# A state-space scan in rounds: another order of work on PE, VectorE and ScalarE, with y's two halves a round apart

## The reference

```python
A = -jnp.exp(A_log)
def step(hst, ins):
    dt_t, B_t, C_t, x_t = ins
    dA = jnp.exp(dt_t[:, :, None] * A)
    hst = hst * dA + (dt_t * x_t)[:, :, None] * B_t[:, None, :]
    y_t = jnp.einsum('bds,bs->bd', hst, C_t)
    return (hst, y_t)
```

## Time and profile before

| | us |
|---|---|
| median of 3 runs | 7119.47 (7112.84 to 7120.07) |
| profiled execution, its own time | 7115.03 |
| span of the profiled execution | 7113.3 |
| PE busy | 6393.6 (90%) |
| VectorE busy | 4188.9 (59%) |
| ScalarE busy | 4613.4 (65%) |
| GpSimd busy | 3331.1 (47%) |
| mean granted clock of PE | 0.932 |

### The profile page before, as it was taken

One profiled execution on the slowest core, in us unless ns is written; L12 is line 12 of the kernel. 1 busy time (PEld: TensorE's weight loads), 2 busy tenths in 40 slices (PEclk: granted clock), 3 DMA queues, 4 the chain that ended last, 5 costly groups with the idle time before them and its releaser, 6 DMA issues. The chain is left out here.

```text
span 7113.3 us, 205317 instructions
## 1 busy us (share of the span) xinstructions
PE 6393.6 (90%) x85792; PEld 3192.1 (45%) x85792; DVE 4188.9 (59%) x6974; ACT 4613.4 (65%) x9618; POOL 3331.1 (47%) x2816
## 2 busy tenths in 40 slices
PE   6888679999999999999999999979899999978988
PEld 3444434444444444444444444434355445444544
DVE  2555556666666666666666666655344445445554
ACT  3555478888888888888888888852244345345554
POOL 0011156666666666666666666640033223224432
PEclk8999879999999999999999999989999999989999
DMA  6555522222222222222222222235200000010000
GB/s 192 150 142 138 159 68 59 59 58 58 65 60 58 59 58 65 60 59 58 59 59 66 59 59 59 58 123 201 95 7 7 10 7 10 4 35 13 10 13 7
DMA packets 596363, 459.87 MB, mean 65 GB/s; under 512 B 449728, under 2 KB 504640, under 8 KB 577280
## 3 DMA queue, kind: packets, MB, share of 16 engines
q1 hardware_dynamic: 594408, 444.73, 21.5%
q10 hardware_dynamic: 1048, 2.16, 0.1%
HBM read 301.29 MB, written 145.49 MB: 63 GB/s over the span
## 5 line engine op out<-in xcount | busy, mean ns | idle before, releaser
L1472 POOL TENSOR_TENSOR s_dec<-s_hs,s_dec 128x512 f32<-128x512 f32 x2040 | 2561.5, 1281 | 1212.7 <-DVE s_hs L1512 791.9
L1393 ACT ACTIVATE s_dec<-s_pa 128x512 f32<-128x512 f32 x4096 | 2268.9, 618 | 403.8 <-PE s_pa L1246 403.6
L1501 DVE TENSOR_TENSOR s_pA<-s_pA,s_dec 128x512 f32<-128x512 f32 x2040 | 1393.0, 694 | 830.3 <-ACT s_hs L1399 563.9
L1512 DVE TENSOR_TENSOR s_hs<-s_pB,s_dec 128x512 f32<-128x512 f32 x2040 | 1330.9, 684 | 338.1 <-PE s_py L1283 236.8
L1283 PE MATMUL s_py<-s_hs,s_cz 128*32 128x256 f32 x16384 | 1392.4, 418 | 0.0
L1399 ACT COPY s_hs<-s_pA 128x512 f32<-128x512 f32 x2048 | 1210.3, 599 | 205.0 <-PE s_pA L1256 201.8
L1292 PE MATMUL s_py<-s_still 128*32 128x512 bf16 x15848 | 1243.2, 386 | 0.0
L1246 PE MATMUL s_pa<-s_dl,s_al 18*128 18x64 bf16 x32768 | 958.9, 192 | 79.7 <-DMA s_dl<-D 48.6
L1256 PE MATMUL s_pA<-az 18*128 18x256 bf16 x4096 | 778.7, 285 | 180.5 <-DVE s_pA L1501 176.5
L1256 PE MATMUL s_pB<-az 18*128 18x256 bf16 x4096 | 826.5, 283 | 3.5 <-DMA az<-U 3.5
L2067 POOL TENSOR_TENSOR t_prob<-t_prob,t_rinv 128x512 f32<-128x512 f32 x512 | 528.7, 1039 | 508.5 <-DVE t_rinv L2440 508.5
(11 more groups left out here) (260 smaller groups left out, 6395.2 us busy)
## 6 DMA issues: line engine op xcount, KB each, us to landing
s_dl<-D SPq DMA_DIRECT2D x512, 144.0 KB
az<-U SPq DMA_DIRECT2D x1024, 72.0 KB
az<-B SPq DMA_DIRECT2D x1024, 36.0 KB
D<-p_dp SPq DMA_DIRECT2D x64, 384.0 KB, 5.8
U<-p_up SPq DMA_DIRECT2D x60, 384.0 KB, 6.3
B<-p_bz SPq DMA_DIRECT2D x144, 128.0 KB, 2.5
SZ<-p_sz SPq DMA_DIRECT2D x16, 1024.0 KB, 4.0
SK<-p_skip SPq DMA_DIRECT2D x16, 1024.0 KB, 5.8
```

Source lines behind the costliest of these rows:

```text
L1393: act.activation(dec[w][:].rearrange("p k i t d -> p (k i t) d")[:, :, DS * q + d:DS * q + d + 8], pa[:, bank, :].rearrange("p (d c) -> p ...
L1472: pool.tensor_tensor(m, two(hs[k][:, (x + 1) % 2, :]), m, ALU.mult).then_inc(m_done, 1)
L1501: dve.tensor_tensor(state, state, of_chunk(k, x), ALU.mult).then_inc(mul, 1)
L1512: dve.tensor_tensor(out, two(pB[:, k - 2, :]), of_chunk(k, x), ALU.add).then_inc(added, 1)
```

## The change

PE's `body`, VectorE's `body` and one wait of ScalarE are rewritten.

- VectorE does, in a normal round, `times` 0, `plus` 3 of the round before, `times` 1, `plus` 2. In x = 0 and 8 `plus` 3 of the round before comes first, ahead of `dec_ready`. One `plus` 3 stands behind the last body.
- PE, in a normal round: `to_a` 0; y of round n-2, half 1; `keep_warm`; `to_b` 3 of this round; `produce` w = 0 with `to_a` 1 beside it; y of round n-1, half 0; `keep_warm`; `produce` w = 1 with `to_b` 2 of the next round beside it. The halves of y are a round apart. x = 0, 8 and x = 1, 9 have orders of their own. `beside` is now called ahead of the products i = 2 and i = 4, and not at the start and at i = 3.
- `keep_warm` writes to `py` only, is called 31 times a body, and still makes two sets.
- ScalarE's `copy_a` of chunk 0 waits also for `y_mm` of 2n-2.

```diff
--- before.py
+++ after.py
@@ -1235,12 +1235,10 @@
             def _(pe):
                 def adt(p, w, banks, beside=None):
 
-                    if beside:
-                        beside(0)
                     wait(pe, taken, 2 * p - 1)
                     for i in range(8):
-                        if beside and i == 3:
-                            beside(1)
+                        if beside and i in (2, 4):
+                            beside(i // 2 - 1)
                         for e in range(2):
                             q, d = 2 * (w[1] % 2) + e, 8 * (w[1] // 2) + i
                             mm = pe.matmul(pa[:, banks[e], DS * i:DS * (i + 1)],
@@ -1285,11 +1283,11 @@
                                        start=(x == 0 and v == 0), stop=(x == BODY - 1), skip_group_check=True)
                     mm.then_inc(y_mm, 1)
 
-                def keep_warm(onto):
+                def keep_warm():
 
                     for _ in range(2):
                         for k in range(CH):
-                            pe.matmul(onto[QR * k:QR * (k + 1), :], still[:, W:W + QR], still[:, 0:W],
+                            pe.matmul(py[QR * k:QR * (k + 1), :], still[:, W:W + QR], still[:, 0:W],
                                       start=False, stop=False, skip_group_check=True)
 
                 def turn_y(p, G, banks):
@@ -1315,58 +1313,77 @@
                     for x in range(BODY):
                         n = BODY * G + x
                         more = not (last and x >= TB)
-                        late = x == 1
-                        before = (x - 1) % BODY
-                        has = not (head and x == 0)
                         ahead = not (last and x == BODY - 1)
-
-                        def to_a0(v):
-                            to_a(n, x, 0, v)
+                        old = (x - 1) % BODY
+
+                        def to_a1(v):
+                            to_a(n, x, 1, v)
 
                         def to_b2(v):
-                            if late and v == 0:
-                                wait(pe, added, 2 * n + 1)
-                                keep_warm(pB[:, 0, :])
                             to_b(n + 1, (x + 1) % BODY, G + (x + 1) // BODY, 2, v)
 
-                        if more and x % TB == 0:
-                            produce(G, x, 0, head, turn, None)
-                            if has:
-                                keep_warm(py)
-                            to_a0(0)
-                            to_a0(1)
-                        elif more:
-                            produce(G, x, 0, head, turn, to_a0)
-                        else:
-                            to_a0(0)
-                            to_a0(1)
-                        for v in range(2):
-                            to_a(n, x, 1, v)
-                        if has and not late:
-                            if x == 9:
-                                wait(pe, c_filled, 2 * G + 2)
-                            y(n - 1, before, 0)
-                            keep_warm(py)
-                        if more:
-                            produce(G, x, 1, head, turn, to_b2)
-                        elif ahead:
+                        def to_b3():
+                            if n:
+                                for v in range(2):
+                                    to_b(n, x, G, 3, v)
+
+                        def make(w, beside):
+                            if more:
+                                produce(G, x, w, head, turn, beside)
+                            elif beside:
+                                beside(0)
+                                beside(1)
+
+                        if x % TB == 0:
+                            if n:
+                                y(n - 2, (x - 2) % BODY, 1)
+                                keep_warm()
+                            to_b3()
+                            make(0, None)
+                            if n:
+                                y(n - 1, old, 0)
+                                keep_warm()
+                            to_a(n, x, 0, 0)
+                            to_a(n, x, 0, 1)
+                            make(1, None)
+                            to_a1(0)
+                            to_a1(1)
+                            if n:
+                                y(n - 1, old, 1)
                             to_b2(0)
                             to_b2(1)
-                        if has and not late:
-                            y(n - 1, before, 1)
-                            if x:
-                                keep_warm(py)
-                        if ahead:
-                            if late:
-                                wait(pe, added, 2 * n + 2)
-                                keep_warm(pB[:, 1, :])
-                            for v in range(2):
-                                to_b(n + 1, (x + 1) % BODY, G + (x + 1) // BODY, 3, v)
-                        if late:
-                            wait(pe, ytok_done, G)
-                            wait(pe, c_filled, 2 * G + 1)
-                            for v in range(2):
-                                y(n - 1, before, v)
+                        elif x % TB == 1:
+                            to_a(n, x, 0, 0)
+                            to_a(n, x, 0, 1)
+                            make(0, None)
+                            to_b3()
+                            if x == 9:
+                                keep_warm()
+                            to_a1(0)
+                            to_a1(1)
+                            if x == 1:
+                                make(1, None)
+                                wait(pe, ytok_done, G)
+                                wait(pe, c_filled, 2 * G + 1)
+                                y(n - 1, old, 0)
+                                keep_warm()
+                                to_b2(0)
+                                to_b2(1)
+                            else:
+                                wait(pe, c_filled, 2 * G + 2)
+                                y(n - 1, old, 0)
+                                keep_warm()
+                                make(1, to_b2)
+                        else:
+                            to_a(n, x, 0, 0)
+                            to_a(n, x, 0, 1)
+                            y(n - 2, (x - 2) % BODY, 1)
+                            keep_warm()
+                            to_b3()
+                            make(0, to_a1)
+                            y(n - 1, old, 0)
+                            keep_warm()
+                            make(1, to_b2 if ahead else None)
                         if x == 2 and not head:
                             turn_y(15 + 33 * G + 6, G, [(12 + e) % BANKS for e in range(2)])
 
@@ -1380,6 +1397,7 @@
                     for v in range(2):
                         to_b(0, 0, 0, k, v)
                 bodies(body)
+                y(BODY * ALL - 2, BODY - 2, 1)
                 y(BODY * ALL - 1, BODY - 1, 0)
                 y(BODY * ALL - 1, BODY - 1, 1)
                 p = 15 + 33 * (ALL - 1) + 17
@@ -1395,6 +1413,8 @@
                         pa[:, bank, :].rearrange("p (d c) -> p c d", d=8), ACT.Exp).then_inc(taken, 1)
 
                 def copy_a(n, x, k):
+                    if k == 0:
+                        wait(act, y_mm, 2 * n - 2)
                     wait(act, bu_a, 2 * n + k + 1)
                     act.copy(hs[k][:, x % 2, :], pA[:, k, :]).then_inc(copied, 1)
 
@@ -1500,15 +1520,17 @@
                         state = two(pA[:, k, :])
                         dve.tensor_tensor(state, state, of_chunk(k, x), ALU.mult).then_inc(mul, 1)
 
-                def plus(n, made, x, k, first):
+                def plus(n, k):
+                    G, x = n // BODY, n % BODY
+                    made = 2 * (n - G // BODIES)
                     wait(dve, bu_b, 2 * n + k - 1)
                     if k == 2:
                         wait(dve, y_mm, 2 * n - 2)
                     out = two(hs[k][:, x % 2, :])
-                    if first:
+                    if n % (BODY * BODIES) == 0:
                         dve.tensor_copy(out, two(pB[:, k - 2, :])).then_inc(added, 1)
                     else:
-                        wait(dve, m_done, made + 2 * x + k - 3)
+                        wait(dve, m_done, made + k - 3)
                         dve.tensor_tensor(out, two(pB[:, k - 2, :]), of_chunk(k, x), ALU.add).then_inc(added, 1)
 
                 def take_y(G):
@@ -1521,15 +1543,19 @@
                     for x in range(BODY):
                         n = BODY * G + x
                         start = first and x == 0
+                        if x % TB == 0 and n:
+                            plus(n - 1, 3)
                         dec_ready(dve, G, x, head)
-                        for k in range(2):
-                            times(n, x, k, start)
+                        times(n, x, 0, start)
+                        if x % TB:
```

(6 more changed lines are left out.)

## The result

| | before | after |
|---|---|---|
| median of the runs | 7119.47 us (3 runs) | 7222.0 us (7219.52 to 7226.81, 3 runs) |
| ratio | | 1.015 (95% interval 1.0136 to 1.0164) |
| span of the profiled execution | 7113.3 us | 7217.7 us |
| mean granted clock of PE | 0.932 | 0.897 |
| a body of the scan | 59.57 us | 61.25 us |

The account below looks back on a forecast made before the run. PE's own work was taken to bound normal rounds, with irregular rounds adding waits and half clock. A body of 18.81 + 10.74 + 8 x 3.15 = 54.75 us against 59.57 saves 303: 7115 - 303 = 6812 us, range 6690 to 7020.

Parts of the forecast that it names:

- the sum: Scan body: 18.81 + 10.74 + 8 x 3.15 = 54.75 us against 59.57, 303 us less in 63 bodies.
- rival 2: PE's clock still falls in x=1: 6.8 us of half clock, 3.2 us a body, total 7014 us; chance 0.20.
- PE's blocks, the normal round: PE's two product blocks in a normal scan round take 0.58 and 0.57 us, the round 3.15, without waits for other engines.
- if no product passed another: PE's matmuls never reorder: each block some 0.02 us longer, 30 us in all, total 6842 us.
- The boundary, the turn, the body: Scan: x=7 to 10 takes 10.74 us, x=15 to 4 18.81, a whole body 54.75.
- The clock: PE's granted clock in the scan was forecast near 1.0.
- the new thin stretch in x=1: PE waits about 1.2 us in 2.5; judged nearer to busy 5.31 of 6.60 (no fall) than 1.52 of 3.50 (fall).
- Rival 4: Slower: idle 0.9 us before turn_y keeps the clock low into x=3 to 5; +76 us, 7191 us; chance 0.05.

Follow-up runs that it names:

- e4: The kernel before with only VectorE's new order, PE and ScalarE unchanged: 7103.7 us, 0.9987 of before.
- e7: e1 with VectorE's order of before (times 0, times 1, plus 2, plus 3): 6914.7 us, 0.9716 of before.
- e8: e1 with one set of zero-weight products instead of two behind y's older half in normal rounds: 6644.7 us, 0.9344 of before.
- e1: The changed kernel with three more keep_warm calls: in x=0 and 8, in x=1, ahead of the turn of y: 6783.6 us, 0.9534 of before.
- e5: The kernel before with two more keep_warm calls in x=1, ahead of and behind to_a 1: 6917.9 us, 0.972 of before.
- e2: The changed kernel with only e1's added keep_warm call in x=0 and 8: 6946.8 us, 0.9763 of before.
- e6: The kernel before without the keep_warm call behind y's second half in x=8: 7117.6 us, 1.0005 of before.
- e10: e1 without its added keep_warm call ahead of the turn of y: 6791.6 us, 0.9548 of before.
- e3: The changed kernel with only e1's added keep_warm calls in x=1 and ahead of the turn of y: 6857.8 us, 0.9638 of before.

## Why the prediction was wrong

The step that failed is the one in the sum that ran every body at full clock, and the weighing of rival 2 that allowed it. The sum put half clock at nothing; the runs showed 16.9 us of it a body, which cost 7.0 us a body and turned a gain of 5.4 into a loss of 1.7.

- **PE's blocks, the normal round: right.** 0.55 and 0.55 against 0.57 and 0.58, 3.11 against 3.15, and no engine makes PE wait there. The alternation costs and brings nothing in these rounds (e4, e7). Nor are the blocks longer, as they would be if no product passed another (6842 us). One set less is worth its full 0.21 (e8), so the round is the sum of PE's blocks.
- **The boundary, the turn, the body: right at the clock they were worked out for.** In e1 x=7 to 10 takes 10.66 us against 10.74, x=15 to 4 18.70 against 18.81, and the body 54.21 against 54.75. The forecast of 6812 us would have been 0.4% off e1's 6783.6. But the 4.8 us a body that it gained were not the order's: e5 gains 3.1 of its own with the old order, by its clock, and the order is worth 2.1. So a good part of the forecast gain hung on the clock, which the prediction did not say.
- **The clock: wrong.** The prediction said that the new thin stretch in x=1 "lies between, nearer the latter", and gave a fall 0.20. It compared busy times, and these do not tell (89% ahead of a fall, 72% ahead of none). It looked at x=1 alone, while the same sequence stands in x=8 and 9, where the change left y's second half without zero products behind it. It noted that the calls fall from 33 to 31 a body and priced them at their own time only; they also helped to hold the clock (e2, e6).
- **The price of rival 2: the size was off.** It had 6.8 us of half clock and 3.2 us a body. Measured are 16.9 us and 61.25 - 54.21 = 7.0. The price for each us was nearly right, 0.40 to 0.45 against 0.47; the number and the length of the falls were not.
- **Rival 4: the right account, the wrong place.** It said that the change is slower from 9.6 us of half clock on. By the measured price the point is (59.57 - 54.21)/0.41 = 13 us, and there were 16.9. But it laid the fall on the wait ahead of `turn_y`, and e10 shows that this wait does no harm.

The books of a body: order -2.2 us (e1 against e5), half clock of after +7.0 (after against e1), half clock of before -3.1, which e5 took out. They are differences of four measured bodies and must add up to the +1.68 measured, so the sum is no proof; what bears it out is the price read inside single traces, which gives 7.2 for the 7.0.

What stays open is which of the removed and moved calls set off which fall. e2 and e3 show that both places count and that they act on each other; e6 shows that one call less in x=8 brings a fall in x=9 in half of the bodies. Why the same work is followed by a fall in one body and not in the next stays open too. A single call in the changed kernel was not tried alone except in x=0 and 8.

## What to carry to other kernels

An order that shortens a PE-bound loop can lose its gain through PE's clock: look at the granted clock by stretch before and after, and price each us of half clock (here 0.4 us). Here filler products cost nothing in the gaps in which PE waits (e1, e5) and their full time where PE is the bound (e8); that is where to put them and where to spare them. Judge a new order at the clock it will have: two calls in the old kernel's gap gave 2.8%, more than the 1.5% that the change took away. And measure the price inside one trace where bodies with and without a fall stand side by side, since nothing else differs between them.

## What the runs showed of the hardware

- PE's granted clock fell after a stretch in which PE was busy 89% of the time (3.05 of 3.41 us), with mostly 18-row products and no wait longer than 0.19 us, and did not after one of 72% (2.38 of 3.30).
- A fall of 10.2 us cost 4.1 us of time in this PE-bound loop, one of 6.8 us 2.8 to 3.1 (e2, e3).
- With the changed kernel the falls came at the same two places in all 63 bodies, 30.7 us apart. In e3 the same work of PE in x=7 to 9, in the same 7.62 us, was followed by a fall in some bodies and by none in most.
- Zero products in PE's waits cost no time: x=15 to 4 takes 18.70 us with and without them (e1, e2).
